# A vision tower on one core: the second norm's tokens turned by a DMA instead of by TensorE, with four reorderings around it

## The reference

```
h = patches(x) @ tok_W                                   # 768 -> 256
u = layernorm(h)
m = gelu(u @ mod_w1 + mod_b1) @ mod_w2 + mod_b2          # 256 -> 1024 -> 256
y = irfft(rfft((u @ in_w + in_b) * m) * rfft(kernel))    # over the 196 tokens of an image
h = h + y @ out_w + out_b
v = layernorm(h)
gate = softmax(v @ router_W.T + router_b), two largest of six, normalised
out = h + v @ base_W.T + base_b + (v @ shared_A.T) @ shared_B.T
        + sum_e gate_e * (v @ routed_A[e].T) @ routed_B[e].T
```

## Time and profile before

| | us |
|---|---|
| three runs | 1212.76, 1216.1, 1300.43 |
| median of the runs | 1216.1 |
| the profiled execution | 1212.12 |
| its span | 1210.3 |
| TensorE matmul busy | 1199.5 (99%) |
| TensorE weight load busy | 1174.2 (97%) |
| VectorE busy | 828.2 (68%) |
| ScalarE busy | 700.0 (58%) |
| GpSimd busy | 401.1 (33%) |

### The profile page before, as it was taken

How to read it: one execution, slowest core, us unless ns; L and a number is a source line. 1 busy time by engine, 2 the same in 40 slices (tenths; PEclk the granted TensorE clock), 3 DMA queues, 4 the chain that set the end, 5 groups by cost and what they waited for, 6 DMA issues and landing times.

```text
span 1210.3 us, 20608 instructions
## 1 busy us (share of the span) xinstructions
PE 1199.5 (99%) x7914; PEld 1174.2 (97%) x7914; DVE 828.2 (68%) x2231; ACT 700.0 (58%) x1287; POOL 401.1 (33%) x459
## 2 busy tenths in 40 slices
PE   8999999999999999999999999999999999999998
PEld 7999999999999999999999999999999999999996
DVE  5567766667766667766677666677666677666777
ACT  7655566555666555665555666556665556665442
POOL 3532244332344232343232443322442423442220
PEclk9999999999999999999999999999999999999999
DMA  7310222211232211222102222212322112221001
GB/s 252 97 38 34 70 71 70 57 31 53 71 70 71 58 27 57 71 70 65 53 25 69 71 71 57 37 47 71 70 70 57 31 54 70 70 70 21 14 14 35
DMA packets 85087, 72.96 MB, mean 60 GB/s; under 512 B 64775, under 2 KB 78958, under 8 KB 81150
## 3 DMA queue, kind: packets, MB, share of 16 engines
q1 hardware_dynamic: 84990, 71.66, 20.8%
...
## 4 chain that ended last, share of the span: by engine, by line
PE 96%; DVE 1%; ACT 1%; DMA 1%; issue 0%; POOL 0%; SPq 0%; DVEq 0%
PE rotating L1424 17%; PE rotating L1425 17%; PE rotating L1426 17%; PE rows_ps L1424 10%; PE rows_ps L1425 10%; PE rows_ps L1426 10%; PE turn L1711 5%; PE turn L1474 2%; PE rows_ps L1484 2%; PE turn L1424 1%; PE turn L1425 1%; PE turn L1426 1%; PE rotating L1555 1%; DMA patches<-dram_x_first 0%; PE turn L1651 0%; DMA prod<-spec_y 0%
## 5 line engine op out<-in xcount | busy, mean ns | idle before, releaser
L522 POOL TENSOR_TENSOR folded<-modulated 128x196 f32<-128x196 f32 x63 | 38.1, 604 | 539.7 <-DVE modulated L1085 539.7
L507 POOL TENSOR_TENSOR gelu_l<-gelu,gelu_h 128x784 fp32r<-128x784 f32 x62 | 122.9, 2001 | 208.7 <-ACT gelu_h L654 208.7
L502 POOL TENSOR_TENSOR patches_l<-patches,patches_h 128x384 fp32r<-128x384 f32 (+1 forms) x186 | 182.1, 1008 | 2.9 <-ACT patches_h L601 2.9
L649 ACT ACTIVATE gelu<-rotating,consts 128x392 f32<-128x392 f32 x256 | 143.0, 585 | 67.9 <-PE rotating L1426 67.5
L1424 PE MATMUL rotating<-x_h,w_h 128*128 128x392 f32 x512 | 176.9, 346 | 0.6 <-ACT gelu L649 0.6
L1424 PE MATMUL rotating<-gelu_h,w_h 128*128 128x392 f32 x512 | 177.4, 347 | 0.0
L1426 PE MATMUL rotating<-x_h,w_l 128*128 128x392 f32 x512 | 174.6, 341 | 0.0
L1425 PE MATMUL rotating<-x_l,w_h 128*128 128x392 f32 x512 | 174.6, 341 | 0.0
L1425 PE MATMUL rotating<-gelu_l,w_h 128*128 128x392 f32 x512 | 174.2, 340 | 0.0
L1426 PE MATMUL rotating<-gelu_h,w_l 128*128 128x392 f32 x512 | 173.9, 340 | 0.0
L1424 PE MATMUL rows_ps<-tokw_h,patches_h 128*128 128x256 f32 x570 | 162.5, 285 | 1.0 <-DVE patches_l L870 1.0
...
## 6 DMA issues: line engine op xcount, KB each, us to landing
...
prod<-spec_y SPq DMA_TRANSPOSE x60, 3.2
...
```

Source lines behind the costliest of these rows:

```text
L502: pool.tensor_tensor(patches_l[:, k, 0:n], patches[:, k, 0:n], patches_h[:, k, 0:n].bitcast(F32), ALU.subtract).then_inc(pool_patches_lo, 1)
L507: pool.tensor_tensor(gelu_l[:, 2 * j:2 * j + 2, :], gelu[:, 2 * j:2 * j + 2, :], gelu_h[:, 2 * j:2 * j + 2, :].bitcast(F32), ALU.subtract)\
L522: pool.tensor_tensor(folded[:, m, 0, :, 1:NF], fwd, back, ALU.add)
L649: act.activation(gelu[:, k, :], bank(g + 1, UP[k])[:, 0:GT], ACT.Gelu, bias=b1_bias[:, k:k + 1]).then_inc(act_gelu, 1)
```

## The change

The second norm is no longer turned by TensorE. VectorE copies the low and the high 16-bit halves of `norm2` apart into `spec_y` (`part_tokens`, 2 copies of 768 elements), SP issues one DMA transpose of 12 blocks into `prod` (`transpose_x2`), VectorE joins the halves back into `norm2`, now turned (`join_x2`, 1 copy of 1536 elements), and `x2_hi` and `x2_lo` read from there. `x2_hi` moves on ScalarE from the end of its round into the next one, between the two halves of `project`. New waits: `fold_halves` of the next round waits for the DMA (`x2_turned`, since both use `spec_y`), and `transpose_fold` waits for `join_x2` (since both use `prod`).

In the same edit `base_route` moves behind two `mlp_up`, the gated turn behind five (its PSUM use changes place with it), `routed` behind seven, `dft` behind eight, `inverse_dft` behind two embedded tiles, the mixer behind the first 3 matmuls of `mlp_down`; ScalarE's gate table goes behind two `gelu_tile`; VectorE's first late `gelu_lo` goes ahead of the transform's products; GpSimd's low parts 0 to 2 go ahead of `fold(mid, 0)`.

```diff
-IN, UP, TURN_GATED, OUT, DOWN = (0, 1), (2, 3, 4, 5, 7, 8, 9, 10), 6, 11, (12, 13)
+IN, UP, TURN_GATED, OUT, DOWN = (0, 1), (2, 3, 4, 5, 6, 8, 9, 10), 7, 11, (12, 13)
...
+            def transpose_x2(d):
+                sp.wait_ge(dve_token_halves, 2 * d + 2)
+                sp.dma_start_transpose(x2_turned_rows, token_halves).then_inc(x2_turned, 16)
...
                 if in_range(i - 3):
                     store(i - 3)
+                if i >= 2:
+                    transpose_x2(i - 2)
...
+                if i + 2 < ROUNDS:
+                    patches_lo(i + 2, (0, 1, 2))
                 fold(mid, 0)
                 if i + 2 < ROUNDS:
-                    patches_lo(i + 2, (0, 1))
+                    patches_lo(i + 2, (3, 4))
                 fold(mid, 1)
                 if i + 2 < ROUNDS:
-                    patches_lo(i + 2, range(2, KT))
+                    patches_lo(i + 2, (5,))
...
                     act.wait_ge(pe_idft, DH * g)
+                    act.wait_ge(x2_turned, 16 * g)
...
+            def x2_hi(d):
+                act.wait_ge(dve_x2_whole, d + 1)
                 for m in range(DH):
-                    act.wait_ge(pe_turn_x2, DH * d + m + 1)
-                    act.activation(hi[:, m, 0:n], ps[:, m, 0:n], ACT.Copy).then_inc(act_x2_hi, 1)
+                    act.activation(x2_h[:, m, :], x2_whole[:, m, :], ACT.Copy).then_inc(act_x2_hi, 1)
...
                     fold_halves(back, 0)
                     project(mid, (0,))
+                    if in_range(tail):
+                        x2_hi(tail)
                     fold_halves(back, 1)
                     project(mid, (1,))
...
+            def part_tokens(d):
+
+                dve.wait_ge(dve_norm2, d + 1)
+                for b in range(2):
+                    dve.tensor_copy(token_parts[:, b], norm_parts[:, b]).then_inc(dve_token_halves, 1)
+
+            def join_x2(d):
+                dve.wait_ge(x2_turned, 16 * (d + 1))
+                dve.tensor_copy(x2_whole_halves, x2_turned_halves).then_inc(dve_x2_whole, 1)
...
-                if in_range(back):
-                    turn_x2(back, rows_ps, norm2)
```

103 lines of the change are left out of this document (55 added, 48 removed).

## The result

| | before | changed |
|---|---|---|
| runs, median | 1214.55 us | 1338.36 us |
| lowest | 1212.76 us | 1335.89 us |
| profiled execution, span | 1210.3 us | 1334.4 us |
| granted TensorE clock | 1.000 | 0.973 |

The changed kernel takes 1.1024 times as long, 95% interval 1.1009 to 1.1039: 124 us slower. Forecast were 1221 us, and 1243 as the upper end. Each median is over four executions, of which one ran in a slower state (1300.43 us before and 1945.17 us changed, the latter at a granted clock of 0.557); the ratio is taken without these two.

The account below looks back on a forecast made before the run. TensorE's instruction stream was taken to bound the 36.72 us round. Waits of 12.2 us over 29 rounds, less 4.8 gained, plus 1.0 at the end, gave +8.4 on 1212.1, rounded up to 1221; range 1207 to 1243, 8 in 10.

Parts of the forecast that it names:

- part 4: VectorE's low part of gelu ahead of the transform's products delays `inverse_dft`: about 0.1 us a round, between 0 and 0.7.
- rival C: At the join: `join_x2` slowed beside GpSimd's low parts by contention for SBUF interfaces shared with VectorE; 1232 us, chance 0.09.
- Part 5: Second norm's chain of copies, DMA, join, high and low parts before `base_route`: 0.1 us a round, between 0 and 0.8.
- Part 6: GpSimd's moved low parts, later `modulate` and fold, ScalarE's table loads cost nothing; about 1.0 us once in the written-out end.
- Part 1: At `project`: second norm's transposes go, the first norm's low part is waited for; net 0.16 us a round, 4.8 gained.
- Parts 2 and 3: Gated turn waits about 0.12 us for the gate; `mlp_up` 6 behind it waits about 0.1 for its bank, each round.
- Rival B: Second norm's DMA lands too late for `base_route`, with ScalarE waiting before `fold_halves`: 1241 us, 1260 with slow copies; chance 0.20.

Follow-up runs that it names:

- e1: Changed kernel with VectorE's first late low part of gelu put back behind the transform's products: 1251.7 us.
- e3: Changed kernel plus eight unused matmuls of 512 columns ahead of `inverse_dft`, where TensorE would wait: 1307.1 us.
- e13: Changed kernel, its order untouched, with GpSimd's two low parts of gelu cut to 4 columns: 1252.6 us.
- e14: e1 with GpSimd's two low parts of gelu cut to 4 columns: 1253.1 us.
- e5: e1 with GpSimd's last low part of the patches waiting until VectorE has both low parts of the second norm: 1231.2 us.
- e8: Kernel before the change with GpSimd's new order of patch low parts and folds alone: 1216.0 us, ratio 1.0022.
- e6: e5 with `TURN_AT` 4 in place of 5, so the first norm's transposes come three matmuls earlier: 1229.8 us.
- e10: e6 with `base_route` behind three `mlp_up`, ScalarE's work reordered, and `join_fold`'s first copy ahead of the gate's logits: 1223.2 us.
- e11: e5 with `base_route` back in its old place ahead of the first `mlp_up`: 1329.8 us.

## Why the prediction was wrong, step by step

**The step that failed is part 4**, "a low part ahead of the products. About 0.1, between 0 and 0.7". The low part was priced as its 0.98 us, from a row in which nothing else ran, and the only question asked was how much of it lay ahead of `dft`'s end. Measured were 3.25 us in the 20 rounds with a fall of the clock (41.08 in the changed kernel less 37.83 in e1) and 1.72 in the other ten, in two pieces:

- The lock: 2.70 in place of 0.97 us. 1.45 of it reached `inverse_dft` in the round read; the rest was spare. I hadn't asked what GpSimd does at that time, though its two `gelu_lo` are in its row of the code. Before, VectorE's low parts stood behind the products, when GpSimd was done.
- The clock: the prediction priced a wait at its own length. Behind this one TensorE's clock fell to 0.50 in 20 rounds, for 1.5 us each. By e3, 31 us of the 124.

What the prediction did work out there, the order alone, was right: it put the low part 0.7 ahead of the end of `dft` (it starts at 678.80, `dft` ends at 679.41) and its cost at 0.1; e13, the same order without the lock, is within 1 us of e14.

The prediction had the lock in view as rival C, at the one place where an operation was new. It should have been asked of every VectorE instruction that the change moves, and of every one whose operand moves from PSUM to SBUF.

**Part 5, the second norm's chain: right in its steps, mis-sized at the last.** The copies took 0.556 each (forecast 0.56), the join 1.06 (1.1), the landing 3.6 (3.85, between 3.2 and 4.8). The 12 blocks are issued in 1.45 and land 0.4 us later than 8 do. The last low parts were taken as 0.5 each behind their high parts, the length that they had when they read PSUM. They now read SBUF, beside GpSimd, and take 2.02 together: `base_route` waits 0.49 (666.61 - 665.77 - 0.18 = 0.66 from start to start), where "0.1, between 0 and 0.8" stood. With GpSimd kept off (e5) the wait goes, and 20.6 us with it.

**Part 6, what costs nothing: wrong in one item of GpSimd's.** Its low parts 0 to 2 ahead of the fold cost nothing in a middle round (e8), and some 2 to 5 us once, in the first (2.4 by the medians, 5.0 in the profiled execution). But the item left the sixth behind the second fold without asking what VectorE does there. That `modulate` and the fold come later was harmless: ScalarE waits 2.22 for the DMA in any case, forecast as "some 2.5".

**Part 1 holds in kind, and gained less.** Each `project` now waits for the first norm's low part, 30 times; from `turn_x1` to `project` are 2.71 and, in the other kind of round, 702.81 - 699.97 = 2.84, as forecast to 0.01. Before, the two were 2.82 and 2.84, so the gain is 0.11 and nothing. The 0.1 more that the prediction added, for a first matmul of `project` slowed by the transposes ahead of it, didn't come: from `project` to the next block are 2.24 before and after. So of the transposes' 0.68 a round 0.06 were had, some 1.7 us in all and not 4.8, and e6 shows that an earlier `turn_x1` doesn't free the rest, since the DMA's landing is next.

**Parts 2 and 3 hold in kind, and were too small.** The six `mlp_up` and the turn behind `base_route` lose 0.21 ahead of the gated turn (673.13 - 669.68 = 3.45 for three, 3.24 before) and 0.25 behind it (2.49 for two, 2.24 before), together 0.46 where 0.22 stood.

With both locks taken out, e5 is the kernel that the prediction thought it was pricing (but for the low part's place, which by e13 and e14 makes less than 1 us): 1231 us against 1221 forecast, in the range. In the profiled executions its 18.7 us over the kernel before are 30 x 0.44 in the rounds, 3.8 at the head and 1.6 at the end, which is the fall of the clock named under e10.

Rival B, the late DMA, was real as a limit (e6, e11) and not as the cause. Rival C had 14.5 us for a slowed join; what happened was C's mechanism at two other places, for 86.6 + 20.6 = 107 us, some 31 of them the clock's.
